# Scan of a hybrid layer stack: the product of carried states and decayed C in three 16-bit passes

## What is computed

```python
        # 2 sequences of 512 tokens; H_SIZE = 512, NH = 128 heads of HD = 64, SS = 128, NG = 8 groups, CHUNK = 128
        cs = jnp.cumsum(dA, axis=-1)
        seg = cs[..., :, None] - cs[..., None, :]
        Lmat = jnp.where(tri, jnp.exp(seg), 0.0)
        xdt = xc * dtc[..., None]
        scores = jnp.einsum('bclhn,bcshn->bchls', Cc, Bc) * Lmat
        Ydiag = jnp.einsum('bchls,bcshp->bclhp', scores, xdt)
        decay_states = jnp.exp(cs[..., -1:] - cs)
        states = jnp.einsum('bclhn,bchl,bclhp->bchpn', Bc, decay_states, xdt)
        chunk_decay = jnp.exp(cs[..., -1])
        def step(carry, inp):
            st, cd = inp
            new = carry * cd[:, :, None, None] + st
            return (new, carry)
        _, prev = jax.lax.scan(step, init, (st_seq, cd_seq))
        Yoff = jnp.einsum('bclhn,bchpn,bchl->bclhp', Cc, prev, jnp.exp(cs))
        Y = (Ydiag + Yoff).reshape(Bsz, S, H, P) + x * D[None, None, :, None]
```

## Time and profile before

| | |
|---|---|
| median of 3 runs | 2455.38 us (2453.66 to 2455.76) |
| profiled execution, its own time | 2454.44 us |
| its span (first to last instruction) | 2452.3 us |
| mean granted clock of TensorE | 0.985 |
| busy: TensorE, VectorE, ScalarE, GpSimd | 96%, 73%, 65%, 56% of the span |
| stage of the scan (from the first slot to the last scan) | 60 to 1515 us |

### The profile page before, as it was taken

The page is one execution under the profiler, slowest core; times in us unless marked ns, Lnnn a source line. Parts: engine busy times, 40 slices in busy tenths (PEclk is TensorE's granted clock), DMA queues, the critical chain, the costliest instruction groups (busy, mean ns, idle before and its releaser), DMA issues. The chain is left out here.

```text
span 2452.3 us, 50016 instructions
## 1 busy us (share of the span) xinstructions
PE 2353.6 (96%) x16008; PEld 1329.6 (54%) x16008; DVE 1782.2 (73%) x3250; ACT 1585.1 (65%) x3327; POOL 1362.0 (56%) x1130
## 2 busy tenths in 40 slices
PE   6999999999999999999999998789999999999897
PEld 3555555555555555555555554355555565555443
DVE  6787777777777777777777784677777777788422
ACT  7776776777777777777777773366555556565422
POOL 4577576576566566567567578433444344454223
PEclk8999999999999999999999999899999999999999
DMA  7343343343343333343333440400110110000000
GB/s 249 108 137 112 113 136 109 112 136 112 111 133 113 112 132 113 112 135 110 122 128 112 136 147 23 196 34 1 44 44 2 44 44 18 27 18 1 1 0 34
DMA packets 113835, 218.91 MB, mean 89 GB/s; under 512 B 9632, under 2 KB 43040, under 8 KB 111360
## 3 DMA queue, kind: packets, MB, share of 16 engines
q1 hardware_dynamic: 113536, 215.28, 26.6%
HBM read 212.10 MB, written 3.15 MB: 88 GB/s over the span
## 5 line engine op out<-in xcount | busy, mean ns | idle before, releaser
L991 ACT ACTIVATE E<-wq,cst 128x128 f32<-128x128 f32 x1024 | 311.7, 389 | 2.3 <-PEq L298 2.3
L256 DVE SCALAR_TENSOR_TENSOR xc<-bank,taps,xc 128x511 f32<-128x511 f32 (+2 forms) x384 | 283.0, 737 | 21.0 <-ACT xc L243 20.5
L1932 POOL TENSOR_TENSOR qT<-qT,qrot 128x512 f32<-128x512 f32 x64 | 81.3, 1270 | 370.8 <-DVE qrot L1822 370.8
L1295 POOL TENSOR_TENSOR acc<-acc,sq 128x512 f32<-128x512 f32 x112 | 165.6, 1478 | 185.4 <-ACT sq L1003 185.3
L61 PE MATMUL bank<-xhi,wx 128*128 128x512 f16 x640 | 242.5, 379 | 0.0
L60 PE MATMUL bank<-xlo,wx 128*128 128x512 f16 x640 | 242.4, 379 | 0.0
L59 PE MATMUL bank<-xhi,wx 128*128 128x512 f16 x640 | 242.3, 379 | 0.0
L1107 DVE TENSOR_TENSOR E<-E,cbm 128x1024 f32<-128x1024 f32 x128 | 234.9, 1835 | 0.9
L1278 POOL TENSOR_TENSOR ecs<-ecs,xcC 128x768 f32<-128x768 f32 x128 | 235.2, 1838 | 0.4 <-POOLq L298 0.4
L1174 DVE SCALAR_TENSOR_TENSOR u<-xc,D,bank 128x512 f32<-128x512 f32 x128 | 95.6, 747 | 184.1 <-PE bank L815 172.1
L1283 POOL TENSOR_TENSOR xw<-xt,wdec 128x384 f32<-128x384 f32 x128 | 106.5, 832 | 178.0 <-DVE xt L1126 177.9
(11 more groups left out here) (246 smaller groups left out, 6591.5 us busy)
## 6 DMA issues: line engine op xcount, KB each, us to landing
wq<-cs_rows SPq DMA_DIRECT2D x128, 512.0 KB, 4.1
ecs<-ecs_rows SPq DMA_DIRECT2D x128, 384.0 KB, 3.5
wx<-in_w_xbc SPq DMA_DIRECT2D x80, 256.0 KB, 2.6
wz<-in_w_z SPq DMA_DIRECT2D x64, 256.0 KB, 2.6
wo<-in_w_o SPq DMA_DIRECT2D x64, 256.0 KB, 4.0
wq<-in_wq SPq DMA_DIRECT2D x8, 1024.0 KB, 5.8
awo<-in_wo SPq DMA_DIRECT2D x8, 1024.0 KB, 4.8
wkv<-in_wkv SPq DMA_DIRECT2D x8, 512.0 KB, 3.6
```

The source lines that it names most:

```text
L256: self.nc.vector.scalar_tensor_tensor(out=dst[:, d:T], in0=self.k.bank[bank][:, 0:T - d], scalar=self.taps[:, bass.ds(g, 1), b, j, 3 - d:4 ...
L991: ins = nc.scalar.activation(E[t.i % 4][:, h, c], sc.csr[t.i % 2][:, h, c * P:(c + 1) * P], ACT.Relu, scale=-1.0, bias=head(sc.cst, t, c, h))
L1295: nc.gpsimd.tensor_tensor(acc[t.b][:], acc[t.b][:], sq[:], ALU.add).then_inc(acc_done, 1)
```

## The change

`scan` multiplies the carried states by the decayed C in three passes of 16 bits: sthi x lead(ecs), sthi x ecslo and stlo x lead(ecs), each for both heads, where one product of 32 bits stood for each head. E times xt stays in 32 bits. The halves are made in these places:

- GpSimd: `ecslo`, the remainder of the decayed C, a new instruction of 768 elements directly behind L1278, waiting for it and for the scan of the tile before (`y_ready`), since there is one buffer.
- ScalarE: `sthi`, a copy of the three states to float16, behind yhi, waiting for the last state.
- VectorE: `stlo`, the remainder, directly behind the masking of E, waiting for `sthi`.
- TensorE waits for `cs_lo` and `st_lo` where it waited for `cs_done`. `st`, `sthi`, `stlo` and `ecslo` have one buffer each; `st` had two.

```diff
-        st = [sb(f"st{i}", [P, CH - 1, P]) for i in range(2)]
+        st = sb("st", [P, CH - 1, P])
+        sthi, stlo = sb("sthi", [P, CH - 1, P], F16), sb("stlo", [P, CH - 1, P], F16)
+        ecslo = sb("ecslo", [P, 2, T - P], F16)
...
                 def scan(t):
                     pe.wait_ge(m_done, t.n + 1)
-                    pe.wait_ge(cs_done, t.n + 1)
+                    pe.wait_ge(cs_lo, t.n + 1)
+                    pe.wait_ge(st_lo, t.n + 1)
                     pe.wait_ge(gz_done, t.n + 1)
...
-                        for h in range(2 if c else 0):
-                            r = slice(h * HD, (h + 1) * HD)
-                            mm = nc.tensor.matmul(Y[r, cols], st[t.i % 2][:, c - 1, r], sc.ecs[t.i % 4][:, h, (c - 1) * P:c * P],
-                                                  start=False, stop=True, skip_group_check=True)
+                        e, d = sc.ecs[t.i % 4], slice((c - 1) * P, c * P)
+                        for x in range(3 if c else 0):
+                            for h in range(2):
+                                r = slice(h * HD, (h + 1) * HD)
+                                mm = nc.tensor.matmul(Y[r, cols], (sthi, sthi, stlo)[x][:, c - 1, r],
+                                                      (lead(e[:, h, d]), ecslo[:, h, d], lead(e[:, h, d]))[x],
+                                                      start=False, stop=x == 2, skip_group_check=True)
...
+                def leading_states(t):
+                    act.wait_ge(s_step, 3 * t.n + 3)
+                    nc.scalar.copy(sthi[:], st[:]).then_inc(st_hi, 1)
...
                     square(s)
                     leading(s)
+                    if tile_at(g, m + 1):
+                        leading_states(tile_at(g, m + 1))
...
+                def rest_of_states(t):
+                    dve.wait_ge(st_hi, t.n + 1)
+                    nc.vector.tensor_tensor(stlo[:], st[:], sthi[:], ALU.subtract).then_inc(st_lo, 1)
...
                         masked(n1)
+                        rest_of_states(n1)
...
                     nc.gpsimd.tensor_tensor(e[:], e[:], sc.xcC[t.b][:, P:T].unsqueeze(1).to_broadcast([P, 2, T - P]),
                                             ALU.mult).then_inc(cs_done, 1)
+                    pool.wait_ge(cs_done, t.n + 1)
+                    wait(pool, y_ready, t.n)
+                    nc.gpsimd.tensor_tensor(ecslo[:], e[:], lead(e[:]), ALU.subtract).then_inc(cs_lo, 1)
```

More of the change, by code:

```diff
@@ L667, in mixer @@
         cs_done, xw_done, acc_done, rstd_done = S("cs_done"), S("xw_done"), S("acc_done"), S("rstd_done")
+        st_hi, st_lo, cs_lo = S("st_hi"), S("st_lo"), S("cs_lo")
         acc_split, xw_lo, bt_done = S("acc_split"), S("xw_lo"), S("bt_done")
@@ L1021, in first @@
                     turned_B(tile_at(0, 0), ring_bank(1, USE_BT))
+                    leading_states(tile_at(0, 0))
                     decays(tile_at(0, 2))
@@ L1112, in state @@
                         dve.wait_ge(st_ready, t.n + 1)
-                        nc.vector.tensor_copy(st[t.i % 2][:, 0], W[:, 0:P]).then_inc(s_step, 1)
+                        nc.vector.tensor_copy(st[:, 0], W[:, 0:P]).then_inc(s_step, 1)
                         return
@@ L1118, in state @@
                         mm = nc.vector.scalar_tensor_tensor(
-                            out=st[t.i % 2][:, c, r], in0=st[t.i % 2][:, c - 1, r], scalar=head(sc.cd, t, c, h),
+                            out=st[:, c, r], in0=st[:, c - 1, r], scalar=head(sc.cd, t, c, h),
                             in1=W[:, c * P + h * HD:c * P + (h + 1) * HD], op0=ALU.mult, op1=ALU.add)
                     mm.then_inc(s_step, 1)
+                def rest_of_states(t):
+                    dve.wait_ge(st_hi, t.n + 1)
+                    nc.vector.tensor_tensor(stlo[:], st[:], sthi[:], ALU.subtract).then_inc(st_lo, 1)
                 def turned_x(t):
@@ L1166, in first @@
                     masked(tile_at(0, 0))
+                    rest_of_states(tile_at(0, 0))
                     turned_x(tile_at(0, 1))
```

## The result

The changed kernel takes 2500.91 us (median of 4 runs, 2498.93 to 2503.22), the kernel before 2454.52 beside it (2452.53 to 2455.76). The ratio is 1.019, with a 95% interval from 1.0172 to 1.0208: slower by 46 us. The profiled execution has a span of 2497.1 us, 44.8 more than before.

A forecast was written before the change was run, and what follows sets the result against it. TensorE was taken to set the scan's pace. Groups +35 us, savings included, and tail +10 make +45 on 2454.4, with 0.9 for the median 2500 us; main case 2475 to 2525, 2456 to 2528 8 times in 10.

The forecast's parts named there:

- TensorE's saving: Scan products on TensorE: three 16-bit passes replace a pair of 32-bit products, saving 0.14 us a tile, 18 us over 128.
- rival 3: Half-width 16-bit products on TensorE don't overlap, adding 0.38 us a tile: 2535 us (2520 to 2555), chance 0.08.
- The price of the new instructions: Per tile: ecslo 1.47 us on GpSimd (other end 1.82), stlo 0.558 on VectorE, sthi 0.471 on ScalarE.
- Taking turns: VectorE instructions with two SBUF inputs and GpSimd's wait for each other; u's gating over 1 us, stlo near 1.2.
- The worked slot: One slot, at 710.77: xt comes 2.1 us later, and TensorE stands 1.2 us for xwlo.
- The group: Sixteen slots between scans: seven gain 0.1 to 0.14 us, nine lose, net +5.2; 7.5 groups, taken as +35.
- The alternative of +25: Groups ahead of the tail: if stlo never has to wait for a queued split, they add 25 us.
- The tail: End of the scan, GpSimd almost without a gap: six ecslo add 8.8 to 11.2 us, taken as +10.
- Behind the last scan: The part of the kernel after the last scan: nothing changes there.
- Rival 2: Only ScalarE's chain to the gate and the tail cost: +4 us, 2459 us (2454 to 2470), chance 0.12.
- Rival 1: New work fits the other engines' reserves, only the tail pays: -8 us, 2447 us, chance 0.10.

The follow-up runs named there:

- e1: Changed kernel with sthi, stlo and ecslo made once, for the first tile, and reused by all tiles: 2436.91 us, 0.992 of the kernel before.
- e6: Changed kernel with stlo moved in VectorE's list from behind the masking of E to behind xt: 2486.72 us, 1.0128 of the kernel before.
- e4: Changed kernel with stlo made as a scaled copy of st, with one SBUF input: 2487.46 us, 1.0126 of the kernel before.
- e5: Changed kernel with the last unit's eight tiles multiplied in 32 bits, without the halves: 2490.94 us, 1.0143 of the kernel before.
- e2: As e1, but ecslo is made for every tile: 2449.42 us, 0.997 of the kernel before.
- e3: Changed kernel with ecslo made once and reused, sthi and stlo made for every tile: 2476.46 us, 1.0086 of the kernel before.
- e11: As e1, but sthi is made for every tile: 2442.30 us, 0.9957 of the kernel before.
- e10: Changed kernel with the states' leading half read in place instead of ScalarE's copy, stlo still behind the masking: 2503.58 us, 1.0197 of the kernel before.
- e7: As e6, and the states' leading half is read in place instead of ScalarE's copy: 2470.89 us, 1.0062 of the kernel before.
- e8: As e7, with three passes only in tiles 3 to 6 and 11 to 14 of a group, none in the last group: 2444.66 us, 0.9959.

## Why the prediction came out as it did

The result lies 1 us from the time predicted. The mechanism is the one forecast; that the sum is met so closely is in part luck, as the terms below show. (2454.4 + 45 is 2499.4, not 2499.9 as the sum has it; with the 0.9 it still gives 2500.)

- **TensorE's saving.** Taken: three passes for two heads at 0.0575 us each, 0.14 us a tile, the scan 1.55 us to the states' first product. Measured: 729.61 to 729.78 for three, 729.13 to 730.67 for the scan, slots of 10.36 instead of 10.51. Alone (e1) the scans are 15 us closer together, where 18 were counted. Right, and rival 3 is out. Loading half-width weights is recorded with 107 to 110 ns, but the two heads overlap.
- **The price of the new instructions.** ecslo 1.47 to 1.82: measured 1.466 at its shortest, 1.793 in the median. stlo 0.558: 0.544. sthi 0.471: 0.496. ecslo was taken at its lower end with turns apart; its mean is 1.66, and GpSimd's busy time rose by 235 us instead of 190. The prediction puts 14 us on the step from 1.47 to 1.82, so 1.66 should have added some 8. The sum doesn't show them: other terms were too high by at least as much.
- **Taking turns.** The gating of u has a mean of 1133 ns, stlo of 1341 with a shortest of 544: both as announced. That the wait depends on what GpSimd is doing is shown by e6, where the same stlo has 0.61, and by the 19 cases of the changed kernel. Its reach was put too narrowly: it is not only instructions with two SBUF inputs (e4).
- **The worked slot.** xt +2.1 and TensorE standing 1.2 us: measured +2.43 and 1.69. The missing 0.3 comes from the gating: ecslo begins 2.56 us after the scan's start, not 2.11, as the late xwlo of the slot before is ahead of it on GpSimd, and holds u to 733.16.
- **The group.** +5.2 us worked out, measured 36.1 / 7 = 5.15; fifteen units 36.7 where +35 was taken. The slots behind the two-split ones: 1.6 and 0.8 worked out, 1.61 and 0.81 in the mean of the seven groups. Of the sixteen slots six gain and ten lose, one of these by 0.03; seven and nine were named. The rest of the sum is right in total and not slot by slot: the slots ahead of a unit's end and its first were to lose 0.6 to 0.9 each and lose 0.03 to 0.71 in the mean, while the second and third of a group, not named, lose 0.85 and 0.40. The alternative of +25, stlo never waiting, is out.
- **The tail.** +10, measured +10.7 by the scans and 10 by e5; the last scan stands behind an ecslo. It was put down to ecslo alone, which has 7.5 to 8.9 of it (e2, e3).
- **Behind the last scan** nothing was to change; it took 3.4 us less in this execution. Over the profiled executions this part goes roughly with the time that TensorE's granted clock stood at its lower level (1.2 GHz) in it: 934.8 us with 39.8 at that level (e11), 937.1 with 46.2 (the changed kernel), 940.5 with 49.5 (before), 945.7 with 61.6 (e10). So single traces are held against each other between the scans, and whole times by their medians (46.4 apart).
- **Rival 2**, ScalarE's chain, is no whole explanation but a part: TensorE's waits for the gate rose from 5.5 to 18.9 us, and with stlo out of the way the copy is worth 16 (e7). Alone it costs 5 us (e11), and in the changed kernel as it is, nothing is gained without it (e10). **Rival 1** fails at the 1.0 us between xwlo and its use, as it was put: TensorE waits there, 43.5 us in all.

What the prediction did not see is how the costs share out: it spoke of ecslo and stlo side by side, but ahead of the tail ecslo alone costs 2.8 us, while stlo costs 34 on top of sthi (e2, e3, e11), and ecslo costs 16 there once sthi and stlo are in place.

One thing stays open: how much of the loss is the waiting for GpSimd, and how much the mere length of stlo in front of xt. No form of stlo of the same length that takes no turns was run, and in e4 the 0.2 us of length alone were worth 13.5 us.

## What to carry to other kernels

Follow a moved or added instruction to the next engine that waits, slot by slot, and not by the busy shares: a 0.54 us instruction on an engine with 2.5 us of reserve was the dearest part here, because what stood behind it fed TensorE. VectorE's work with two inputs in SBUF, or with one at doubled pace, waits for GpSimd's running instruction, so its place in the queue matters as well as its length. A cost measured alone is no constant: the same 0.5 us copy cost 0, 5 and 16 us in three settings. Where a saving on TensorE has its price on others, buy it only in the slots that have room: placing and reading the halves better brought 46 us of loss down to 15 (e7), and keeping the passes to 56 of 128 tiles turned that into 11 of gain (e8).

## What the runs showed of the hardware

- 16-bit products into the two halves of the columns: a pair of them every 0.0575 us, the time of one full-width product, though each half-width load is recorded with 107 to 110 ns. The step from the last pair to the first full-width product takes 0.17 us, 0.11 more than that pace (730.50 to 730.67); whether the change of width does it, or the wait that stands there, is not shown.
- VectorE's one-input scaling of 384 f32 elements to f16 takes 346 ns at its shortest and waits for GpSimd's instruction as a two-input one does (up to 1.97 us); reading only every second half-word leaves both as they are. The statistics instruction, one SBUF input at plain pace, doesn't wait (658 to 696 ns), nor does u = D x + Y, with one input in SBUF and one in PSUM (716 to 750 ns).
- GpSimd waits for VectorE too: xw lasts 0.83 us, at most 0.84, where stlo stands ahead of xt, and 0.99 in the mean, at most 1.14, where stlo is queued beside it (e6).
